# A two-stage convolution kernel put into one interleaved stage: a new sample order, two loads of every sample, band matrices on GpSimd, the output bias inside the expansion

## The chip, the cores and the metric

One core of a Trainium2 chip. The metric is the device time of one execution in microseconds; the kernel before took 1702.09 us, the median of three runs (1700.39 to 1702.37).

## What is computed

x has the shape (16, 64, 64, 768): 16 samples, 64 x 64 pixels, 768 channels, float32, 12.6 MB a sample. For each sample:

```
xn   = group_norm(x)                      # 32 groups of 24 channels, moments over all pixels of the sample
xc   = conv1x1(xn, conv1_w) + conv1_b      # 768 -> 16 channels
h    = mean(xc over pixels) @ H_w.T + H_b  # 4 logits a sample
g    = softmax over the top 2 of h         # (16, 4)
E_i  = downsample(conv3x3(upsample(xc, 2**i), convl_w) + convl_b),  i = 0..3
out  = x + conv1x1(sum_i gw[i, b] * E_i, conv2_w) + conv2_b
gw   = reshape(g, (4, 16))                 # a reshape, not a transpose
```

The reshape matters for the order of the work: the four gates of sample b come from row b // 4 of g's flat order, that is from the samples b//4, 4 + b//4, 8 + b//4 and 12 + b//4. Outputs of the samples 0 to 3 need the projections of 0, 4, 8 and 12, and no others.

## The kernel before

Everything runs on one core. A sample lies in SBUF as eight slots of 128 partitions x 3072 floats (1536 KB), each slot of four tiles of 128 pixels x 768 channels. There are twelve slots (x_low with 8, x_high with 4).

**First stage, all samples in order** (project_sample, copy_sample, take_stats, fold_norm). SyncE loads the slots; a load waits until the slot's last tenant is transposed. VectorE takes bn_stats of 30 of the 32 groups of a pair of slots (a chunk; four chunks a sample), ACT takes the other two groups by activations with accumulation. TensorE sums the moments over partitions with a matmul per chunk, and fold_norm turns them into scaled weights w1 by a dozen small VectorE instructions. For each of 24 steps (chunk c, block k of 128 channels) TensorE does eight transposes (L403) into one of three PSUM banks, ACT copies them to xT (L533), and TensorE projects them with four matmuls (L413) into img_ps. Transposes run LEAD = 6 steps ahead of projections, into the next sample too; statistics of the next sample run beside the projection of this one. ACT copies the 16-channel image with its bias to xc (L559), which keeps all 16 images. The loop turns over three samples at a time.

**Middle.** Logits, softmax and gates for all samples; the taps of the four experts; weights for the output.

**Second stage, samples 15, 0, 1, ..., 14** (expand_sample, add_sample, split_sample, store_and_reload). The last sample is still in SBUF, the other 15 are loaded again. Per sample VectorE weighs the taps (L820, L822) and makes seven band matrices (L828); TensorE convolves with 35 matmuls (70 records, L473), a quarter behind each of the slots 3 to 6 of the sample before. ACT and VectorE split the result into a high and a low float32r half (L599, L850), TensorE spreads them (L486, L487), ACT copies them to es4 (L603). For each of 32 tiles TensorE does four matmuls: two that write the output bias (L500, ones times b2) and two with the expansion (L501), 512 and 256 columns each. VectorE adds the tile to x in its slot (L867), and SyncE stores a slot when its four tiles are added, then reloads it (L321, L265). Eight slots are in use; the queue holds a wait for each.

SyncE issues all transfers, in program order, on one queue: a transfer whose wait is not met holds back those behind it. In the same way each engine works through its own order.

Of the kernel before, what the change touches and what calls it, by code (L numbers as in the profile page):

```python
# [12 lines left out]
P = 128  # L27
B, HH, WW, D = 16, 64, 64, 768
R, E = 16, 4
G = 32  # L30
# [6 lines left out]
TILES = HH * WW // P  # L37
SPS = TILES // QN
CHUNKS = SPS // 2
SLOTS = 12  # L40
LOW = 8
TURNS = 3
LOOPS = (B - 1) // TURNS
STEPS = CHUNKS * KB
XT_PS = 3
XT = 6
LEAD = KB
GV = G - 2
STATS_BUFS = 2
HALF = 2 * QN * CG // 2  # L50
SUMS_AT = [4, 9, 14, 19]

SCALAR_AT = [at + g for at in (1, 6, 11, 15) for g in range(G - GV)]
FOLD_OPS = 9
AHEAD_SUM = 4
AHEAD_DEVIATION = 3
AHEAD = AHEAD_SUM + AHEAD_DEVIATION + 8
GN_EPS = 1e-5
# [7 lines left out]
MAT_MASK = [SAME, SAME, SAME, ABOVE, BELOW, FIRST, LAST]  # L66

# [28 lines left out]
def slot_place(i):  # L96

    return (i // 2) % 2, 2 * (i // 4) + i % 2


# [15 lines left out]
MAT_ORDER = [HERE, UP, DOWN, FROM_ABOVE, FROM_BELOW, TOP, BOTTOM]  # L116

MATS_AT = 2
MATS_BEFORE = [MAT_ORDER[:1], MAT_ORDER[1:3], MAT_ORDER[3:5], MAT_ORDER[5:]]

CONV = [(m, a) for m in MAT_ORDER for a in (MID, LEFT, RIGHT, LEFT_EDGE, RIGHT_EDGE)]


def program(nc, x, conv1_w, conv1_b, convl_w, convl_b, conv2_w, conv2_b, H_w, H_b, out):
# [3 lines left out]
    coef = resize_taps()  # L128

    ctx = ExitStack()  # L130
    scratch = ExitStack()
    with ctx:
# [5 lines left out]


        x_low = sb("x_low", [P, LOW, QN, D])  # L140
        xc = sb("xc", [P, B, PIX])
        ident = sb("ident", [P, P])
        pooled = sb("pooled", [P, B])
        small = sb("small", [P, 3, G])


        x_high = sb("x_high", [P, SLOTS - LOW, QN, D], stack=scratch)
        xT = sb("xT", [P, XT, QN, 2 * P], stack=scratch)
        unread_copy = sb("unread_copy", [P, 2 * QN, CG], BF16, stack=scratch)
        w1T = sb("w1T", [P, KB, R], stack=scratch)  # L150
        w1_first = sb("w1_first", [P, KB, 2, 2 * R], stack=scratch)
        group_sum = sb("group_sum", [P, G], stack=scratch)
        group_of = sb("group_of", [P, 2, KB // 2, G // 2], stack=scratch)
        picked = sb("picked", [P, 2, KB // 2, G // 2], stack=scratch)


        stats = sb("stats", [P, STATS_BUFS, G, 6], stack=scratch)
# [50 lines left out]
        def slot(n):  # L208
            return x_low[:, n] if n < LOW else x_high[:, n - LOW]

# [51 lines left out]
        def _(sp):  # L262
# [3 lines left out]

            def load_sample(loop, turn, first):

                for i in range(SPS):
# [627 lines left out]
```

## Time and profile before

| | before |
|---|---|
| median of three runs | 1702.09 us |
| span of the profiled execution | 1703.1 us |
| its own time | none is listed beside the span |
| moved | 390.60 MB read, 201.33 MB written |
| mean | 348 GB/s |
| granted TensorE clock, mean | 0.909 |

The span goes from the first to the last instruction. "Busy" of TensorE is modelled from its pipelined instructions. The DMA share is the mean busy share of the core's 16 DMA engines; in saturated stretches it reads 1.02 to 1.03, since packets overlap a little. Times are in microseconds from the span's start.

### The profile page before, as it was taken

How to read it: one execution, taken by the hardware profiler on the slowest of the kernel's cores; microseconds unless marked ns; L12 is line 12 of the kernel's file. 1: busy time of each engine (PE TensorE's matmuls, PEld its weight loads, DVE VectorE, ACT ScalarE, POOL GpSimd, SP SyncE). 2: the span in 40 equal slices, each digit the busy share in tenths (PEclk: the TensorE clock that was granted, in tenths of full speed). 3: DMA queues.
4: the chain of work that ended last, by engine and by line, in shares of the span. 5: the costliest groups of instructions: out<-in, count | busy, mean ns of one | idle time of the engine just before them, and what ended most of it. 6: DMA issues, size and time to landing. Idle time of an engine off the chain costs nothing.

```text
span 1703.1 us, 28023 instructions
## 1 busy us (share of the span) xinstructions
PE 1399.3 (82%) x9584; PEld 991.1 (58%) x9584; DVE 1188.5 (70%) x3092; ACT 528.5 (31%) x1028; POOL 8.1 (0%) x28
## 2 busy tenths in 40 slices
PE   2799999999999999788897688778768767868862
PEld 2566666666666666466665466556556555656652
DVE  6988888788879887657666656655665664655642
ACT  3577777677777777300000000000000000000000
POOL 0000000000000001000000000000000000000000
PEclk7899999999999999889999898889799879879876
DMA  9888888788888882049999999999999999999999
GB/s 361 315 302 315 313 316 315 275 315 304 298 312 317 301 317 93 1 176 410 416 415 415 417 415 415 417 415 412 415 414 411 403 402 402 402 405 410 399 409 367
DMA packets 203029, 593.24 MB, mean 348 GB/s; under 512 B 10290, under 2 KB 10290, under 8 KB 202932
## 3 DMA queue, kind: packets, MB, share of 16 engines
q1 hardware_dynamic: 202932, 591.95, 89.3%
q8 instruction: 60, 0.98, 0.2%
q14 instruction: 37, 0.30, 0.1%
HBM read 390.60 MB, written 201.33 MB: 348 GB/s over the span
## 4 chain that ended last, share of the span: by engine, by line
PE 48%; DMA 28%; SPq 13%; DVE 6%; issue 3%; ACT 1%; DVEq 0%; ACTq 0%
PE xT_ps L403 22%; DMA out<-x_low 19%; PE img_ps L413 13%; DMA x_low<-in_x 9%; SPq L321 7%; SPq L265 6%; PE img_ps L473 5%; PE xT_ps L500 3%; DVE x_low L867 3%; PE xT_ps L501 2%; PE misc_ps L423 2%; DVE stats L678 2%; ACT xc L559 1%; ACT xT L533 0%; DVE taps L822 0%
## 5 line engine op out<-in xcount | busy, mean ns | idle before, releaser
L867 DVE TENSOR_TENSOR x_low<-x_low,xT_ps 128x768 f32<-128x768 f32 x512 | 470.2, 951 | 322.5 <-PE xT_ps L501 191.0
L500 PE MATMUL xT_ps<-b,all_one 128*128 128x512 f32 (+1 forms) x1024 | 430.5, 424 | 205.3 <-DVE x_low L867 204.6
L533 ACT COPY xT<-xT_ps 128x1024 f32<-128x1024 f32 x384 | 387.4, 1009 | 174.3 <-PE img_ps L413 172.2
L678 DVE BATCH_NORM_STATS2 stats<-x_low 128x6 f32<-128x192 f32 x1320 | 355.9, 344 | 68.6 <-DMA x_low<-in_x 51.4
L500 PEld LDWEIGHTS xT_ps<-b,all_one 128*128 128x128 f32 x1024 | 226.3, 221 | 281.0 <-DVE x_low L867 232.4
L501 PE MATMUL xT_ps<-w,es 128*128 128x512 f32 (+1 forms) x1024 | 376.6, 384 | 0.0
L403 PE MATMUL xT_ps<-ident,x_low 128*128 128x128 f32 x2112 | 291.9, 283 | 24.8 <-DMA x_low<-in_x 11.5
L403 PEld LDWEIGHTS xT_ps<-ident,x_low 128*128 128x128 f32 x2112 | 235.1, 143 | 117.2 <-ACT xT L533 60.4
L599 ACT ACTIVATE es_hi<-img_ps,bias_es 128x512 fp32r<-128x512 f32 x16 | 11.0, 688 | 799.1 <-PE img_ps L473 799.1
L501 PEld LDWEIGHTS xT_ps<-w,es 128*128 128x128 f32 x1024 | 231.5, 226 | 30.6
L473 PE MATMUL img_ps<-xc,band 128*128 (+6 forms) x1120 | 219.4, 343 | 4.2 <-DVE band L828 4.2
L473 PEld LDWEIGHTS img_ps<-xc,band 128*128 128x128 f32 x1120 | 157.4, 196 | 67.3 <-issue 62.9
L678 DVE BATCH_NORM_STATS2 stats<-x_high 128x6 f32<-128x192 f32 x600 | 162.0, 344 | 11.7 <-DMA x_high<-in_x 11.5
L413 PE MATMUL img_ps<-xT,xc 128*32 128x256 f32 x1920 | 153.4, 391 | 8.4 <-ACT xc L559 8.4
L403 PE MATMUL xT_ps<-ident,x_high 128*128 128x128 f32 x960 | 130.0, 278 | 0.0
L403 PEld LDWEIGHTS xT_ps<-ident,x_high 128*128 128x128 f32 x960 | 104.4, 141 | 41.6 <-ACT xT L533 28.0
L413 PE MATMUL img_ps<-xT,w_first 128*32 128x256 f32 x1152 | 92.3, 396 | 2.1 <-ACT xc L559 2.1
L828 DVE TENSOR_TENSOR band<-taps,masks 128x640 f32<-128x640 f32 x112 | 87.6, 820 | 0.6
L413 PEld LDWEIGHTS img_ps<-xT,xc 128*32 128x32 f32 x1920 | 37.8, 108 | 49.3 <-issue 32.5
L603 ACT CAST es<-xT_ps 128x512 fp32r<-128x512 f32 x64 | 34.6, 589 | 70.1 <-PE xT_ps L487 70.1
L423 PE MATMUL misc_ps<-stats,ones 128*128 128x192 f32 x128 | 39.2, 391 | 20.6 <-ACT xc L551 7.7
L423 PEld LDWEIGHTS misc_ps<-stats,ones 128*128 128x128 f32 x128 | 20.0, 196 | 46.5 <-issue 24.7
(105 smaller groups left out, 432.5 us busy)
## 6 DMA issues: line engine op xcount, KB each, us to landing
x_low<-in_x SPq DMA_DIRECT2D x208, 1536.0 KB, 11.8
out<-x_low SPq DMA_DIRECT2D x128, 1536.0 KB, 18.0
x_high<-in_x SPq DMA_DIRECT2D x40, 1536.0 KB, 9.9
x_high<-in_L_conv_conv_w SPq DMA_DIRECT2D x8, 48.0 KB, 10.2
bias<-in_L_conv_conv_b SPq DMA_DIRECT2D x8, 0.1 KB, 9.9
wl_raw<-in_L_conv_convl_w SPq DMA_DIRECT2D x8, 9.0 KB, 1.9
bias_l<-in_L_conv_convl_b SPq DMA_DIRECT2D x8, 0.1 KB
gate_w<-in_L_conv_H_w SPq DMA_DIRECT2D x8, 0.2 KB
```

The lines of the kernel that those rows point to most:

```text
L265: sp.dma_start(slot(n), x_v[sample, p, j]).then_inc(loaded[n], 16)
L321: sp.dma_start(out_v[sample, p, j], slot(i)).then_inc(stored[i], 16)
L403: last = nc.tensor.transpose(xT_ps[:, buf, q, half * P:(half + 1) * P], slot((SPS * turn + 2 * c + half) % SLOTS)[:, q, k * P:(k + 1) * P] ...
L413: last = nc.tensor.matmul(img_ps[32 * q:32 * q + 32, 2 * P * (c // 2):2 * P * (c // 2 + 1)], w1[turn][:, k, c % 2, :], xT[:, n % XT, q, :] ...
L423: nc.tensor.matmul(misc_ps[:, 0:6 * G], ones[:, :], stats[:, c % STATS_BUFS].rearrange("p g t -> p (g t)"), start=(c == 0), stop=(c == CHU ...
L473: last = nc.tensor.matmul(img_v[:, blk_out, col_out], band[:, m, ax].rearrange("p h r -> p (h r)"), xc_v[:, order, blk_in, col_in], start= ...
L500: nc.tensor.matmul(add_ps[:, n % 2, part], all_one[:, :], b2[:, part], start=True, stop=False)
L501: last = nc.tensor.matmul(add_ps[:, n % 2, part], es4[:, q, j * P:(j + 1) * P], w2[:, p, part], start=False, stop=True)
L533: nc.scalar.copy(xT[:, n % XT], xT_ps[:, n % XT_PS]).then_inc(xT_copied, 1)
L678: ins = nc.vector.bn_stats(stats[:, c % STATS_BUFS, g, :], tiles[:, :, g * CG:(g + 1) * CG])
L828: nc.vector.tensor_tensor(band[:, m], taps[:, MAT_ROW_TAP[m]].unsqueeze(2).broadcast_to(full), masks[:, MAT_MASK[m]].unsqueeze(1).broadcas ...
L867: nc.vector.tensor_tensor(slot(i)[:, q, :], slot(i)[:, q, :], add_ps[:, n % 2, :], ALU.add).then_inc(added, 1)
```

## The change

The two stages become one list of 22 units, and all loops are written out. A unit (a, b) projects sample a and makes the output of sample b side by side; either can be None. One function, orders(), writes the order of TensorE, ACT and VectorE; the order of the transfers is written out by hand. L is the first load of a slot, R its second, S its store; "L4.0:0" loads slot 0 of sample 4 into place 0 of 12.

```diff
+UNITS = [(4, None), (8, None), (12, None), (0, None), (1, 0), (2, 1), (3, 2), (9, 3), (13, None), (5, None),
+         (6, 5), (7, 6), (14, 7), (10, 4), (11, 10), (15, 11), (None, 15), (None, 8), (None, 9), (None, 12),
+         (None, 13), (None, 14)]
+KEPT = {}
+TRANSFERS = """
+L4.0:0 L4.1:1 L4.2:2 W1 L4.3:3 L4.4:4 L4.5:5 L4.6:6 L4.7:7 L8.0:8 L8.1:9 L8.2:10 L8.3:11 L8.4:6
...
+L6.7:8 R5.1:10 R5.2:3 R5.3:4 L7.0:6 R5.4:8 S5.0 S5.1 L7.1:5 R5.5:11 S5.2 L7.2:9 L7.3:10 S5.3
+R5.6:3 L7.4:0 R5.7:1 S5.4 L7.5:4 S5.5 L7.6:2 R6.0:7 L7.7:8 S5.6 R6.1:11 S5.7 R6.2:3 R6.3:1
+L14.0:2 R6.4:8 S6.0 S6.1 L14.1:0 R6.5:4 S6.2 L14.2:7 L14.3:11 S6.3 R6.6:3 L14.4:9 R6.7:10 S6.4
+L14.5:1 S6.5 L14.6:5 R7.0:6 L14.7:8 S6.6 R7.1:4 S6.7 R7.2:3 R7.3:10 L10.0:5 R7.4:8 S7.0 S7.1
...
+S15.7 R8.3:6 R8.4:7 R8.5:11 S8.0 S8.1 S8.2 S8.3 S8.4 S8.5 R8.6:5 R8.7:10 R9.0:3 R9.1:9
+R9.2:1 S8.6 S8.7 R9.3:4 R9.4:0 R9.5:8 R9.6:2 S9.0 S9.1 S9.2 S9.3 S9.4 S9.5 S9.6
```

The sizes, and the order of the steps (chunk 3, the slots 6 and 7, is transposed first):

```diff
-XT = 6
-LEAD = KB
-GV = G - 2
-STATS_BUFS = 2
+XT = 4
+LEAD = 2
+XC = 6
+BANDS = 4
+GV = G - 4
+TILE_PAIRS, TILE_PAIRS_LOADED = 10, 12
+GROUPS_FROM, GROUPS_FROM_LOADED = 6, 4
+LATE_SUM_PART = 4
+def step_chunk(n):
+    return CHUNKS - 1 - n // KB, n % KB
```

The body of orders(), for one unit. "late" holds where this unit and the sample are both in play: then the last chunk's statistics, the fold and the first two transposes of a stand at the start of its own unit.

```diff
+    def tile(b, t):
+        pe.append(("tile", b, t))
+        dve.append(("add", b, t))
+        if t == 13:
+            spread(b, 2)
+        if t == 15:
+            spread(b, 3)
...
+        if due is not None:
+            pe.append(("logits", due))
+            act.append(("exponent", due))
+            dve.append(("softmax", due))
+            dve.append(("gates", due))
+        if is_late:
+            for c in range(CHUNKS - 1):
+                pe.append(("sum", a, c))
+            statistics(a, CHUNKS - 1, range(GV))
+            fold(a)
+        if due is not None:
+            pe.append(("gates", due))
+        if b is not None:
+            for part in range(NM):
+                pe.append(("conv", b, part))
+                if is_late and part == LATE_SUM_PART:
+                    pe.append(("sum", a, CHUNKS - 1))
+            act.append(("high", b))
+            dve.append(("low", b))
+            for part in range(2):
+                spread(b, part)
+        if is_late:
+            for n in range(LEAD):
+                transpose(a, n)
+        if a is None:
+            for t in range(TILES):
+                tile(b, t)
+            continue
+        per_pair, groups, done, summed = tiles_by_pair(u), groups_by_pair(u), 0, 0
+        for m in range(STEPS // 2):
+            tiles = list(range(done, done + per_pair[m]))
+            done += per_pair[m]
+            for place, n in enumerate((2 * m + LEAD, 2 * m + LEAD + 1, 2 * m, 2 * m + 1)):
+                if place >= 2:
+                    pe.append(("project", a, n))
+                elif n < STEPS:
+                    transpose(a, n)
+                elif following is not None and not late(u + 1):
+                    transpose(following, n - STEPS)
+                for t in tiles[place * len(tiles) // 4:(place + 1) * len(tiles) // 4]:
+                    tile(b, t)
...
+            for c in range(CHUNKS):
+                part = [g for of, g in groups[m] if of == c]
+                if part:
+                    statistics(following, c, part)
```

So a unit's 32 tiles are spread over its 12 pairs of steps, 84 groups of the next sample's first three chunks over pairs 4 to 11. Transposes, tiles and spreads share three PSUM banks in turn (ring_ps, three of 1024 columns). The loads and stores, TensorE's tile and GpSimd's bands:

```diff
+            def load(kind, s, i):
+                n, _, before = loads[kind, s, i]
+                if before is not None:
+                    was, s0, i0 = before
+                    if was == "L" and i0 >= KEPT.get(s0, 0):
+                        sp.wait_ge(transposed, AI[s0] * STEPS + (CHUNKS - i0 // 2) * KB)
+                    else:
+                        sp.wait_ge(stored[n], 16 * stores[n])
+                sp.dma_start(x_sb[:, n], x_v[s, i // 4, i % 4]).then_inc(loaded[n], 16)
...
-                    for part in (slice(0, 512), slice(512, D)):
-                        nc.tensor.matmul(add_ps[:, n % 2, part], all_one[:, :], b2[:, part], start=True, stop=False)
-                        last = nc.tensor.matmul(add_ps[:, n % 2, part], es4[:, q, j * P:(j + 1) * P], w2[:, p, part],
-                                                start=False, stop=True)
+                for part in (slice(0, 512), slice(512, D)):
+                    last = nc.tensor.matmul(flat_ps[:, buf, part], es4[:, q, (i % 4) * P:(i % 4 + 1) * P], w2[:, part],
+                                            start=True, stop=True)
...
+            def weigh_taps(b, bi):
...
+                for e in range(E):
+                    g, of_e = gates[:, b, e:e + 1], experts[:, e].rearrange(flat)
+                    if e == 0:
+                        link(nc.gpsimd.tensor_scalar(all_e, of_e, g, None, ALU.mult))
+                    else:
+                        part = band[:, NM * bi % BANDS].rearrange("p a h r -> p (a h r)")[:, 0:NT * NT * R]
+                        link(nc.gpsimd.tensor_scalar(part, of_e, g, None, ALU.mult))
+                        link(nc.gpsimd.tensor_tensor(all_e, all_e, part, ALU.add))
...
+                    nc.gpsimd.tensor_tensor(band[:, n % BANDS], taps[:, MAT_ROW_TAP[m]].unsqueeze(2).broadcast_to(full),
+                                            masks[:, MAT_MASK[m]].unsqueeze(1).broadcast_to(full),
+                                            ALU.mult).then_inc(band_ready, 1)
```

The output bias sits in rows 64 to 127 of w2, against rows of es4 that are kept at one. es4 has the spread values in its first 64 partitions only, and is copied in four parts of 64 x 1024. The expert taps are computed on GpSimd too. xc keeps six images. ACT takes four groups of a chunk, VectorE 28. Gates are computed in four rounds, when a = 0, 5, 10 and 15 is projected.

## Rows read from the trace of the kernel before

**Rows 1.** The page: busy time of each engine over the span.

```profile
PE 1399.3 (82%) x9584; PEld 991.1 (58%) x9584; DVE 1188.5 (70%) x3092; ACT 528.5 (31%) x1028; POOL 8.1 (0%) x28
```

**Rows 2.** Projections of line 413: durations, first and last start.

```profile
L413 PE MATMUL img_ps<-xT,w_first x1152: 379/379/637, 55.0 to 703.6; 128*32 128x256 f32 x192
```

**Rows 3.** Stretches: length, busy PE, PEld, DVE, ACT, POOL, then clock, DMA share, GB/s.

```profile
20.00:45.00 25.00, 4.34 (x20) 2.86 (x18) 23.73 (x94) 7.00 (x26) 0.00 (x0) 0.58 1.03 387
...
58.00:700.00 642.00, 624.37 (x6130) 403.07 (x6128) 535.38 (x2180) 462.75 (x901) 5.28 (x14) 0.99 0.76 283
708.00:733.00 25.00, 17.48 (x74) 11.93 (x75) 15.40 (x30) 0.69 (x1) 0.00 (x0) 0.70 0.00 1
...
800.00:1340.00 540.00, 422.20 (x1874) 320.84 (x1875) 343.30 (x404) 25.54 (x45) 0.00 (x0) 0.89 1.03 415
1340.00:1690.00 350.00, 256.35 (x1100) 196.43 (x1099) 199.86 (x231) 14.19 (x25) 0.00 (x0) 0.84 1.02 404
```

**Rows 4.** Waits in total: us, times, longest; the last row the DMA queue's.

```profile
PE xT_ps L500 <- DVE x_low L867: 204.6, 141, 6.2
DVE x_low L867 <- DMA x_low<-in_x: 131.2, 43, 8.0
...
SPq L265 <- DMA out<-x_low: 340.4, 58, 8.2
```

**Rows 5.** Timeline of the first stage: start, length, engine, line; a step and a fold.

```profile
643.55 1.09 PE L403 MATMUL xT_ps<-ident,x_high 128*128 128x128 f32 x8
...
644.57 0.64 PE L413 MATMUL img_ps<-xT,xc 128*32 128x256 f32 x8
...
645.14 1.09 PE L403 MATMUL xT_ps<-ident,x_high 128*128 128x128 f32 x8
...
648.33 0.59 PE L423 MATMUL misc_ps<-stats,ones 128*128 128x192 f32 x2
...
652.45 7.89 DVE L678 BATCH_NORM_STATS2 stats<-x_low 128x6 f32<-128x192 f32 x30 [1.28 <-DMA x_low<-in_x]
...
665.63 0.36 DVE L711 TENSOR_REDUCE small<-misc_ps 128x96 f32<-128x192 f32 x1 [5.00 <-PE misc_ps L423]
...
668.99 0.42 DVE L737 TENSOR_TENSOR w_first<-w1T,of_channel 128x96 f32<-128x96 f32 x2
```

**Rows 6.** Timeline at a turn of the first stage's loop.

```profile
550.77 1.09 PE L403 MATMUL xT_ps<-ident,x_low 128*128 128x128 f32 x8 [2.28 <-issue]
```

**Rows 7.** Timeline of the second stage, at full clock: one tile, and a quarter convolution.

```profile
795.15 0.50 PE L500 MATMUL xT_ps<-b,all_one 128*128 128x512 f32 x1 [0.16 <-DVE x_low L867]
...
796.03 0.51 PE L500 MATMUL xT_ps<-b,all_one 128*128 128x512 f32 x1
...
808.42 5.51 PE L473 MATMUL img_ps<-xc,band 128*128 x18
```

**Rows 8.** Groups by line: count, then busy us and mean ns, then idle before.

```profile
L867 DVE TENSOR_TENSOR x_low<-x_low,xT_ps 128x768 f32<-128x768 f32 x512 | 470.2, 951 | 322.5 <-PE xT_ps L501 191.0 <-DMA x_low<-in_x 131.2
...
L828 DVE TENSOR_TENSOR band<-taps,masks 128x640 f32<-128x640 f32 x112 | 87.6, 820 | 0.6
...
L355 POOL TENSOR_SCALAR_AFFINE_SELECT masks<-masks 128x128 f32<-128x128 f32 x10 | 3.6, 358 | 0.7
...
L375 POOL MEMSET masks<- 128x640 f32 x1 | 0.6, 632 | 0.0
```

**Rows 9.** Timeline of the middle: first tap, first convolution, low half.

```profile
711.10 0.42 DVE L820 TENSOR_SCALAR taps<-experts,gates 128x400 f32<-128x400 f32 x1
...
714.45 15.93 PE L473 MATMUL img_ps<-xc,band 128*128 128x512 f32 x70 [4.24 <-DVE band L828]
...
731.24 0.75 DVE L850 SCALAR_TENSOR_TENSOR es_lo<-img_ps,bias_es,es_hi 128x512 fp32r<-128x512 f32 x1 [7.15 <-ACT es_hi L599]
```

**Rows 10.** Timeline of the start: first loads issued, first statistics.

```profile
0.81 3.40 SPq L265 DMA_DIRECT2D x_low<-in_x  x4
...
11.48 7.89 DVE L678 BATCH_NORM_STATS2 stats<-x_low 128x6 f32<-128x192 f32 x30 [11.48 <-DMA x_low<-in_x]
```

More of the change, by code:

```diff
@@ L113, in blk_ranges, with row_due, late @@
             BOTTOM: (slice(NB - 1, NB), slice(NB - 1, NB))}[m]
[L116 to L121, printed above, removed]
+def step_chunk(n):
+    return CHUNKS - 1 - n // KB, n % KB
+def row_due(u):
+    a = UNITS[u - 1][0] if u else None
+    return a // 5 if a is not None and a % 5 == 0 else None
+def late(u):
+    return u < len(UNITS) and None not in UNITS[u]
@@ new lines, in tiles_by_pair, with groups_by_pair @@
+def tiles_by_pair(u):
+    b = UNITS[u][1]
+    if b is None:
+        return [0] * (STEPS // 2)
+    last = TILE_PAIRS if KEPT.get(b, 0) else TILE_PAIRS_LOADED
+    ends = [min(TILES, -(-TILES * (m + 1) // last)) for m in range(STEPS // 2)]
+    return [end - start for start, end in zip([0] + ends, ends)]
+def groups_by_pair(u):
+    a, following = UNITS[u][0], (UNITS[u + 1][0] if u + 1 < len(UNITS) else None)
+    out = [[] for _ in range(STEPS // 2)]
+    if following is None or a is None:
+        return out
+    chunks = 3 if late(u + 1) else 4
+    b = UNITS[u][1]
+    first = 0 if b is None else GROUPS_FROM if KEPT.get(b, 0) else GROUPS_FROM_LOADED
+    last = 12 if late(u + 1) else 11
+    every = [(c, g) for c in range(chunks) for g in range(GV)]
+    for n, item in enumerate(every):
+        out[first + n * (last - first) // len(every)].append(item)
+    return out
@@ new lines, with psum_turns, image_places @@
+PE_ORDER, ACT_ORDER, DVE_ORDER = orders()
+def psum_turns():
+    turn = {}
+    for work in PE_ORDER:
+        if work[0] in ("transpose", "tile", "spread", "weights_2", "logits"):
+            turn[work] = len(turn)
+    return turn
+TURN = psum_turns()
+TURNS = list(TURN)
+def image_places():
+    place, before, free, held = {}, {}, [(n, None) for n in range(XC)], {}
+    for a, b in UNITS:
+        if b is not None:
+            free.append((held.pop(b), b))
+        if a is not None:
+            place[a], before[a] = free.pop(0)
+            held[a] = place[a]
+    return place, before
@@ L630, in expert_taps @@
+            for part in range(2):
+                ins = nc.gpsimd.tensor_tensor(row_kind[:, part:part + 1], masks[:, SAME, part, 0:1],
+                                              masks[:, SAME, 2 + part, 0:1], ALU.add)
+            ins.then_inc(masks_ready, 1)
             def expert_taps():
@@ new lines, in _ @@
+            for work in DVE_ORDER:
+                if work[0] == "groups":
+                    groups(*work[1:])
+                elif work[0] == "add":
+                    add(*work[1:])
+                elif work[0] == "fold":
+                    fold(*work[1:])
+                elif work[0] == "low":
+                    low_half(*work[1:])
+                elif work[0] == "softmax":
+                    softmax(*work[1:])
+                elif work[0] == "gates":
+                    take_gates(*work[1:])
+                elif work[0] == "weights_1":
+                    weights_1()
+                else:
+                    weights_2()
```

1055 lines of the change are left out of this document (539 added, 516 removed).

## The prediction

> **What bounds the kernel now.** I read, in this order, busy time by engine, the stretches of the span, the waits of the engines and of the DMA queue, then single operations in the timeline. The whole-span shares say little, since the kernel has two stages with different limits [rows 1]. In the first, from the first projection at 55.0 us to the last at 703.6 us [rows 2], TensorE is busy 624 of 642 us at a granted clock of 0.99, while the DMA engines stand at 0.76 [rows 3]: 648.6 / 16 = 40.5 us a sample, TensorE's own work. In the middle nothing moves for some 30 us: DMA share 0.00 [rows 3]. In the second stage the DMA share is 1.03 at 415 GB/s, later 1.02 at 404 [rows 3]; TensorE waits 205 us for additions, VectorE 131 us for loads, and the queue itself waits 340 us for stores to free slots [rows 4]. That stage is bound by transfers: 16 of 1.573 MB (1536 KB) a sample, 3.79 us each at 415 GB/s, 60.6 us. So one stage is TensorE's and one is the DMA's, and the change lays the first over the second.
>
> **Prices of a transfer.** Reads alone, with DMA share 1.03, ran at 387 GB/s [rows 3]: 4.06 us each. Alternating reads and stores cost 3.79, so a store is worth 2 x 3.79 - 4.06 = 3.52. A unit that loads a sample, reloads another and stores it has two reads per store: (2 x 4.06 + 3.52) / 3 = 3.88 us, bounded by 3.79 and 4.06. The changed kernel moves 256 loads and 128 stores (8 loads more than before). If the DMA never idled that would be 256 x 4.06 + 128 x 3.52 = 1490 us; all depends on how long it idles.
>
> **Units.** UNITS has 22: six with a projection only (4, 8, 12, 0, 13, 5), ten with both, six with an output only.
>
> *Projection only.* A step is 8 transposes and 4 projections, 1.59 us from one to the next, 24 of them 38.2 us; four moment sums at about 0.52 make 40.3 [rows 5]. The fold, statistics to weights, is 665.63 to 669.41, 3.8 us [rows 5]. Before, six transpose steps ran ahead of it; now the last sum stands behind the last projection and only two steps are ahead, two more transposes cover 2.0 us, and some 2.2 us of TensorE idle remain: 42.5 us a unit. VectorE needs only 4 x 7.4 + 4.8 = 34 us (30 groups take 7.89 us [rows 5], 28 take 7.4). The DMA would need 8 x 4.06 = 32.5, so it idles 10 us in each. The deleted loops save a little: at a turn of the loop TensorE stood 2.28 us [rows 6]; there are three such places, so at most 7 us. I count nothing. The Trainium skill (Runtime: NRT & Kernel Launch, Instruction fetch mechanics) says why: code is fetched strictly ahead in blocks and a taken branch can fall outside them, while straight code hides its fetches. The trace agrees so far that the loop's bodies show no such stall.
>
> *Both.* TensorE: 40.3 for the projection; convolution 9.6 (18 of 70 matmuls, 2873 of 4992 columns, in 5.51 us [rows 7]); tiles: four matmuls with 1536 columns take 796.03 - 795.15 = 0.88 us [rows 7], so two with 768 about 0.44, 32 of them 14; spreads 16 x 0.29 = 4.6: together 68.5. Removing the bias matmuls halves the tile, 14 us a sample of TensorE time, but TensorE was not the limit where they stood. VectorE: 4 x 7.4 for groups, 32 x 0.92 = 29.4 for additions (470.2 / 512 [rows 8]), 5 for fold and low half: 64. The ACT engine (copies, twice the groups, es4) stays near 45. Transfers: 24 x 3.88 = 93. On busy times alone the DMA bounds this unit at 93 us.
>
> But a serial stretch is added, and here I choose. Twelve slots hold the eight of sample a and four of b. In the hand-written order every unit ends: load a'.7, store, load, store, two loads; then the next transfer is load a''.0, which needs the slot of a'.6, free only after six transpose steps of the next unit. Those can't begin before all of a' is loaded and its last two slots are through statistics, fold and, by program order on VectorE and TensorE, the low half and two spreads. From the landing of a'.7: groups 7.4; scaling, semaphores and the moment matmul (0.59 [rows 5]) 1.3; fold 3.8; low half 0.75 [rows 9] and hand-overs 1.1; two spreads 2.0: 15.6 us. Then six transpose steps with two projections and three tiles: 6 x 1.02 + 2 x 0.57 + 3 x 0.44 = 8.6, and 0.9 for the three shared PSUM banks: 9.5. From issue to data the idle queue costs 2.4 (two slots, the first issued at 0.81, are there at 11.48 [rows 10]: 10.7 - 8.1). From a''.0 to a''.7 lie 19 transfers in the table, 73.7 us. Cycle: 15.6 + 9.5 + 2.4 + 73.7 = 101.2 us. After a'.7 five transfers are left, 19.4 us, against 27.5 of the stretch: DMA idle 8 us a unit. Inside the 19 I find no stall: store b.6 and the transposes of chunk 0 are each ready some 10 us before their place.
>
> The granted clock adds to it. After 10 us of idle TensorE the convolution at 714.45 took 15.93 us [rows 9], against 9.6 at full clock: 6.3 more. TensorE idles before the spreads and waits for tiles at a unit's end, so the stretch costs 0 to 7 us more; in the second stage the mean clock was 0.84 to 0.89 [rows 3], nearer to the good end. I take 3: T = 104.
>
> *A gate row is due* ahead of units with b = 0, 5, 10 and 15. From the last projection (703.6) to VectorE's first tap (711.10) are 7.5 us [rows 2, 9]. Then GpSimd weighs taps in seven linked operations of 400 elements and makes five bands before the last moment sum. The trace has no tensor_tensor on GpSimd. From below, a memset of 640 elements takes 0.63 us; from above, affine_select of 128 takes 0.358, 1.79 for 640 in proportion [rows 8]; VectorE's own was 0.82 per band. I take 1.3 per band and 0.85 per weighing, between them (5.95 + 6.5 = 12.5, bounds 6 and 17). With part four 2.3, sum 1.0, fold 3.8, low 1.1, spreads 1.8: 30 us from last projection to first transpose. At b = 10 it replaces 21, so 9 more; at b = 15 the DMA has a backlog. In the other units the first bands are made during the unit before, and the last three lie beside 5.7 us of convolution: nothing. The Trainium skill (GPSIMD Engine Reference, 3.1 Elementwise — side-by-side cycle accounting) has 4497 ns for 2048 elements, two inputs, by which I estimate 1.4 us a band; no run here shows it yet.
>
> *Output only.* 16 x 3.79 = 60.6 us of transfers against 14 of convolution, halves and copy and 29.4 of additions. The slots let loads run during the first part. It stays transfer-bound as before.
>
> **The sum, against the profiled execution** (span 1703.1 us; no other time is listed for it, and it stands 1 us above the median of the runs, 1702.09). First projection at 52 (55.0, less four chunks with two fewer groups and the groups that stood inside the first fold). Four units of 42.5, and 2 for the second weights: 224. Gate row 30: 254. Three cycles of 104: 566. Unit (9, 3) ends by the landing of its 18th transfer, 12 + 70, then groups and fold, 92: 658. Two units of 42.5: 743. Gate row 30: 773. Three cycles: 1085. One with 9 more: 1198. One more: 1302. Then 108 transfers are left (R11.4 on): 10 + 108 x 3.79 + 8 for the last addition and its store = 427: 1729. Less 1: 1728 us.
>
> So the merged stages gain the middle gap and nearly all of the first stage's DMA idling by share, but lose it again: six units at 10, eight boundaries at 11, start and gates.
>
> **Rivals.**
> 1. *The queue stays fed* (not slower). In-flight loads cover the boundary and T is the bare 93. For it: in the second stage a DMA share of 1.02 to 1.03 was held with eight slots only [rows 3]. Against it: slot a'.6 is needed first and comes last. 1729 - 8 x 11 - 9 = 1632. It decides from a stretch under 19 us.
> 2. *TensorE at the lower clock* through each stretch and the transposes that free slots: T = 111, 8 x 7 = 56 more: 1785. For it 15.93 against 9.6 us [rows 9, 7]; against it the mean clock of 0.84 to 0.89 [rows 3].
> 3. *GpSimd is much slower* than its rows (5 us a band): then convolution waits everywhere, about 10 us a unit over 13 more units with outputs: 1859.
> 4. *Code fetch*. By the skill's rule above loops cost and straight code doesn't: 1721 by the three stalls of 2.28 us.
>
> **Chances.** Forecast, with rival 4, 0.53 (own range 1690 to 1770: rate of a transfer 3.79 to 4.06 is -14 to +27, clock -24 to +32, GpSimd +-15); rival 1 0.29; rival 2 0.12; rival 3 0.06. Range: 1632 to 1790. 0.2% (3.4 us) is about what can be told from no change. Faster: rival 1, and 0.06 of the forecast's low end, 0.35. Same 0.05. Slower 0.60.
>
> **What would show it.** The DMA share in mixed units 0.90 to 0.93 with a hole of 8 to 11 us at each boundary; about 104 us from unit to unit; TensorE's spreads waiting for the low half behind the fold; units without output 42.5 us; the last 400 us at 415 GB/s. I am wrong if the share stays at 1.0 across boundaries (rival 1), if slots of b rather than a.6 are awaited, or if band operations take over 2 us.

## The result and the profile after

The changed kernel takes 1813.2 us (median of four runs, 1809.4 to 1815.9) against 1702.2 (1700.4 to 1703.1): ratio 1.0663, 95% interval 1.0638 to 1.0688. It is slower, as forecast, but by 111 us where 26 were forecast, and 23 us above the upper end of the range. The profiled execution has a span of 1809.0 us and a granted clock of 0.839.

The page of the changed kernel, to be laid beside [rows 1] and [rows 3]; in the strips each character is 45.2 us:

```profile
PE 1264.0 (70%) x8700; PEld 856.3 (47%) x8700; DVE 1072.3 (59%) x2763; ACT 668.1 (37%) x1549; POOL 351.8 (19%) x359
...
PEclk9999888888887878978798787977888899768876
DMA  9698719979698888928959789795796999999998
GB/s 364 233 359 313 279 65 409 362 278 410 233 411 343 346 320 314 341 75 321 411 225 411 305 339 411 276 410 237 274 409 267 413 408 414 406 413 412 412 411 358
```

TensorE is busy 135 us less than in [rows 1], with half of each tile's matmuls gone, and the kernel is no faster for it. The DMA strip shows why: full slices alternate with gaps, twice down to 65 and 75 GB/s (the gate rows), and only from 1402 us on does it stay near 411, up to the last slice. Laid over the transfers one by one, the queue moves nothing for 12 to 18 us at each boundary of two units, for 43 us at each of the two full gate rows and for 31 us at the third. One unit with both, cut into its stretches (columns as in [rows 3]):

```profile
899.00:926.00 27.00, 19.88 (x82) 13.10 (x83) 16.58 (x48) 5.01 (x19) 18.58 (x14) 0.76 0.65 259
926.00:934.00 8.00, 8.00 (x72) 6.62 (x71) 2.86 (x3) 5.49 (x6) 0.22 (x1) 1.00 0.00 0
934.00:990.00 56.00, 42.62 (x329) 29.12 (x327) 34.41 (x76) 24.90 (x52) 0.00 (x0) 0.85 1.01 393
990.00:1010.00 20.00, 9.00 (x63) 5.36 (x62) 13.67 (x35) 5.79 (x20) 0.00 (x0) 0.83 1.03 412
1010.00:1037.00 27.00, 18.48 (x83) 12.62 (x84) 17.88 (x54) 5.02 (x19) 18.77 (x14) 0.77 0.71 282
```

The last load of the coming sample (its slot 7) lands at 898.9 and again, one unit on, at 1011.3. From 934 to 1010 the DMA is full (1.01 and 1.03), as forecast; in the 27 us behind a landing it runs out (0.65), and it stands at 0.00 while six transpose steps empty slots. Now those 27 us in the timeline (start, length, engine, line, idle before):

```profile
899.02 0.24 DVE L929 SCALAR_TENSOR_TENSOR stats<-stats 128x56 f32<-128x56 f32 x1
899.17 7.36 DVE L925 BATCH_NORM_STATS2 stats<-x_sb 128x6 f32<-128x192 f32 x28
...
899.31 1.00 PE L696 MATMUL misc_ps<-stats,ones 128*128 128x192 f32 x2 [5.54 <-DVE stats L929]
...
900.11 13.25 PE L734 MATMUL img_ps<-xc,band 128*128 128x512 f32 x50
...
913.21 0.57 PE L696 MATMUL misc_ps<-stats,ones 128*128 128x192 f32 x2
...
913.82 0.36 DVE L935 TENSOR_REDUCE small<-misc_ps 128x96 f32<-128x192 f32 x1 [6.35 <-PE misc_ps L696]
914.07 1.03 POOL L626 TENSOR_TENSOR taps<-taps,band 128x400 f32<-128x400 f32 x1
914.22 0.93 DVE L937 TENSOR_TENSOR norm<-small 128x32 f32<-128x32 f32 x1
915.07 0.18 DVE L938 TENSOR_TENSOR norm<-small 128x32 f32<-128x32 f32 x1
...
920.06 1.77 DVE L956 TENSOR_TENSOR w<-w1T,of_channel 128x96 f32<-128x96 f32 x2
920.20 6.03 POOL L639 TENSOR_TENSOR band<-taps,masks 128x640 f32<-128x640 f32 x4
921.87 0.75 DVE L995 SCALAR_TENSOR_TENSOR es_lo<-img_ps,bias_es,es_hi 128x512 fp32r<-128x512 f32 x1
...
922.72 0.66 PE L751 MATMUL ring_ps<-es_hi,pick 128*64 128x512 f32 x1 [6.81 <-issue]
...
926.02 3.66 PE L673 MATMUL ring_ps<-ident,x_sb 128*128 128x128 f32 x32
```

To be read upward from 926.02. The first transposes stand behind eight spreads (3.3 us), these behind the low half, this behind a fold of 8.0 us (913.82 to 921.87; 3.8 in [rows 5]), this behind the last moment sum at 913.21. That sum is queued on TensorE behind 50 convolution matmuls of 13.25 us, and they are queued behind the third moment sum at 899.31, which waited 5.54 us for the statistics of the third chunk. VectorE was through with the last chunk at 907.5 and then waited 6.35 us for a sum that TensorE could not reach.

Four things therefore lie in the stretch: the hold in front of the convolution, the convolution, the fold and the low clock. The experiments take the fold, the hold, the loads and the clock one by one; the convolution itself was not shortened in any run.

### The profile page after: what moved, and what is told of

Its sections match the earlier page's. It is cut to its first block, busy times and chain, and to the rows that moved or that the text cites. A ratio compares the mean times of both kernels' runs of the same rounds, so it can differ in the third digit from the quotient of the medians.

```text
span 1809.0 us, 23732 instructions
## 1 busy us (share of the span) xinstructions
PE 1264.0 (70%) x8700; PEld 856.3 (47%) x8700; DVE 1072.3 (59%) x2763; ACT 668.1 (37%) x1549; POOL 351.8 (19%) x359
## 4 chain that ended last, share of the span: by engine, by line
PE 44%; DMA 22%; DVE 17%; ACT 6%; issue 5%; SPq 3%; POOL 2%; ACTq 0%; DVEq 0%; POOLq 0%
DMA x_sb<-in_x 22%; PE ring_ps L673 13%; PE img_ps L734 11%; DVE x_sb L1005 8%; PE img_ps L686 7%; PE ring_ps L763 7%; DVE stats L925 6%; PE ring_ps L751 2%; ACT unread_squares L820 2%; PE ring_ps L752 2%; ACT unread_copy L822 2%; SPq L489 2%; ACT xT L803 1%; PE misc_ps L696 1%; SPq L498 1%
## 5 line engine op out<-in xcount | busy, mean ns | idle before, releaser
L1005 DVE TENSOR_TENSOR x_sb<-x_sb,ring_ps 128x768 f32<-128x768 f32 x512 | 470.1, 950 | 353.4 <-PE ring_ps L763 274.4
L925 DVE BATCH_NORM_STATS2 stats<-x_sb 128x6 f32<-128x192 f32 x1792 | 477.1, 344 | 135.3 <-DMA x_sb<-in_x 134.9
L763 PE MATMUL ring_ps<-w,es 128*128 128x512 f32 (+1 forms) x1024 | 339.2, 426 | 291.8 <-ACT xT L803 190.8
L803 ACT COPY xT<-ring_ps 128x1024 f32<-128x1024 f32 x384 | 367.9, 1013 | 189.8 <-PE ring_ps L673 189.4
L673 PE MATMUL ring_ps<-ident,x_sb 128*128 128x128 f32 x3072 | 409.0, 291 | 32.3 <-DMA x_sb<-in_x 18.1
L673 PEld LDWEIGHTS ring_ps<-ident,x_sb 128*128 128x128 f32 x3072 | 378.3, 151 | 73.5 <-issue 44.9
L763 PEld LDWEIGHTS ring_ps<-w,es 128*128 128x128 f32 x1024 | 177.3, 216 | 442.2 <-ACT xT L803 208.6
L639 POOL TENSOR_TENSOR band<-taps,masks 128x640 f32<-128x640 f32 x112 | 168.9, 1533 | 847.1 <-PE img_ps L734 845.8
L734 PE MATMUL img_ps<-xc,band 128*128 128x1 f32 (+8 forms) x1120 | 236.4, 365 | 45.2 <-POOL band L639 45.2
L686 PE MATMUL img_ps<-xT,w 128*32 128x256 f32 x3072 | 235.2, 407 | 11.0 <-DVE w L956 10.6
L686 PEld LDWEIGHTS img_ps<-xT,w 128*32 128x32 f32 x3072 | 73.8, 112 | 100.4 <-ACT xT L803 39.0
L935 DVE TENSOR_REDUCE small<-misc_ps 128x96 f32<-128x192 f32 x16 | 5.7, 358 | 106.8 <-PE misc_ps L696 106.8
## 6 DMA issues: line engine op xcount, KB each, us to landing
x_sb<-in_x SPq DMA_DIRECT2D x256, 1536.0 KB, 14.6
```

Source lines behind the costliest of these rows:

```text
L639: nc.gpsimd.tensor_tensor(band[:, n % BANDS], taps[:, MAT_ROW_TAP[m]].unsqueeze(2).broadcast_to(full), masks[:, MAT_MASK[m]].unsqueeze(1). ...
L673: last = nc.tensor.transpose(ring_ps[:, buf, q, half * P:(half + 1) * P], slot("L", a, 2 * c + half)[:, q, k * P:(k + 1) * P], ident[:, :])
L686: last = nc.tensor.matmul(img_ps[32 * q:32 * q + 32, 2 * P * (c % 2):2 * P * (c % 2 + 1)], w1[:, AI[a] % 2, k, c // 2, :], xT[:, at % XT, ...
L734: last = nc.tensor.matmul(img_v[:, blk_out, col_out], band[:, n % BANDS, ax].rearrange("p h r -> p (h r)"), xc_v[:, XC_PLACE[b], blk_in, c ...
L763: last = nc.tensor.matmul(flat_ps[:, buf, part], es4[:, q, (i % 4) * P:(i % 4 + 1) * P], w2[:, part], start=True, stop=True)
L803: nc.scalar.copy(xT[:, at % XT], ring_ps[:, TURN["transpose", a, n] % RING]).then_inc(xT_copied, 1)
```

## The experiments

Each is compared with the kernel before on the same chip; "cycle" is the time between the high halves (es_hi) of two neighbouring units with both, without the one that holds a gate row. There are seven. In the changed kernel they are 110.8 to 112.4, 111.7 on the mean. "The stretch" goes from the landing of slot 7 to the first transposes: 27.1 us at 899.

**GpSimd's work moved off the fold.**

```
     pool.wait_ge(band_used, NM * bi - BANDS + 1)
+    pool.wait_ge(lo_ready, bi)
     weigh_taps(b, bi)
```

> GpSimd starts to weigh the taps of the next output only when VectorE has taken the low half of the present one, so that no GpSimd work lies beside the fold. Theory (the changed kernel's cycle is the landing of L a.7, then a serial stretch of 25 us up to the next transposes, six transposes, 19 transfers; the fold in it takes 8.0 us instead of 3.8 because GpSimd and VectorE hold each other up): fold back to 3.8 to 4.5 us, its ten occurrences shorter by 4 us each beside an output, of which 8 or 9 count: 1775 to 1785 us. Rival (the order of the transfers or ACT's waits set the time, the fold is off the path): within 5 us of 1813.

1786.7 us, ratio 1.0504 (1.0486 to 1.0522), 26 us less than the changed kernel, just above what I expected; cycle 107.0 to 108.7, 108.0 on the mean. The timeline has the same instructions with nothing beside them:

```profile
899.33 0.36 DVE L936 TENSOR_REDUCE small<-misc_ps 128x96 f32<-128x192 f32 x1 [4.86 <-PE misc_ps L697]
899.72 0.19 DVE L938 TENSOR_TENSOR norm<-small 128x32 f32<-128x32 f32 x1
...
902.61 0.16 DVE L955 TENSOR_TENSOR bias<-bias,sums 128x1 f32<-128x1 f32 x1
902.68 0.42 DVE L957 TENSOR_TENSOR w<-w1T,of_channel 128x96 f32<-128x96 f32 x2
903.14 0.75 DVE L996 SCALAR_TENSOR_TENSOR es_lo<-img_ps,bias_es,es_hi 128x512 fp32r<-128x512 f32 x1
```

The fold is 3.8 us again, from 899.33 to 903.14. So GpSimd beside VectorE cost 4.2 us a fold. In the changed kernel seven of the ten folds beside an output are that long; the three ahead of a gate row have no weighing beside them and take 3.8. The cycle is 3.7 us shorter on the mean.

**The first three moment sums behind part 4 of the convolution.**

```
-        for c in range(CHUNKS - 1):
-            pe.append(("sum", a, c))
...
     if is_late and part == LATE_SUM_PART:
-        pe.append(("sum", a, CHUNKS - 1))
+        for c in range(CHUNKS):
+            pe.append(("sum", a, c))
```

> In the units with both, the moment sums of the first three chunks stand with the fourth behind part 4 of the convolution, so that the convolution starts with the image and not with the third chunk's statistics. Theory: convolution starts about 6 us earlier, the last moment sum comes some 4 us earlier in the seven or so units where no gate row is due: 1780 to 1790 us. Rival (the convolution isn't on the path, the stretch is VectorE's): no change.

1790.1 us, ratio 1.0521 (1.0499 to 1.0542), 23 us less; cycle 106.8 to 109.7, 108.7 on the mean. The hold in front of the convolution is real, and this run understates it. The fold now starts 9.8 us behind the landing of slot 7 (893.3), where it was 14.9 in the changed kernel. But it lies beside more of GpSimd's bands and takes 9.7 us (903.14 to 912.83) instead of 8.0:

```profile
903.14 0.36 DVE L934 TENSOR_REDUCE small<-misc_ps 128x96 f32<-128x192 f32 x1 [0.69 <-PE misc_ps L695]
...
906.17 6.04 POOL L638 TENSOR_TENSOR band<-taps,masks 128x640 f32<-128x640 f32 x4
...
907.84 1.44 DVE L945 TENSOR_TENSOR norm<-norm,small 128x32 f32<-128x32 f32 x1
909.20 1.62 DVE L947 TENSOR_TENSOR picked<-norm,group_of 128x96 f32<-128x96 f32 x1
...
912.83 0.75 DVE L994 SCALAR_TENSOR_TENSOR es_lo<-img_ps,bias_es,es_hi 128x512 fp32r<-128x512 f32 x1
```

So 5 us are won ahead of the fold and 1.6 lost in it.

**The last load of a sample one place earlier, and one place later.** In the eight units with the pattern below; the first line is the changed kernel, then the two edits.

```
 L.6 R.0 L.7 S.6
 L.6 L.7 R.0 S.6     earlier
 L.6 R.0 S.6 L.7     later
```

> In the table of transfers, L a.7 changes places with the load of the other sample directly before it, in eight units; the transfers are the same. Theory: one transfer fewer between the first transposes and the landing of L a.7, 3.9 us in each of eight cycles: 1780 to 1785 us. Rival (what bounds is the rate of the DMA, or the waits for additions and stores): no change, since the same bytes move in the same time.

> The changed kernel, with slot 7's load one place later in eight units (behind the store of slot 6 instead of ahead of it): the opposite of the run in which it stood one place earlier and nothing came of it. Theory (the landing of slot 7 and the end of VectorE's groups of chunk 2 stood at the same moment, so earlier gains nothing, but later costs): 4 to 5 us in each of eight cycles, 1843 to 1855 us. Rival (the places of these transfers don't matter): within 5 us of 1813.

Earlier: 1818.5 us, ratio 1.0686 (1.0663 to 1.0710). Later: 1817.7 us, 1.0683 (1.0668 to 1.0699). Both are some 5 us above the changed kernel, with intervals that overlap its own. An earlier load gained nothing and a later one cost hardly anything: my theory of a critical slot 7 falls. Of the second kernel, around the last chunk:

```profile
1017.10 0.24 DVE L926 SCALAR_TENSOR_TENSOR stats<-stats 128x56 f32<-128x56 f32 x1
1020.75 7.36 DVE L922 BATCH_NORM_STATS2 stats<-x_sb 128x6 f32<-128x192 f32 x28 [3.42 <-DMA x_sb<-in_x]
1028.14 1.22 DVE L926 SCALAR_TENSOR_TENSOR stats<-stats 128x56 f32<-128x56 f32 x1
...
1031.31 0.57 PE L693 MATMUL misc_ps<-stats,ones 128*128 128x192 f32 x2
...
1031.92 0.36 DVE L932 TENSOR_REDUCE small<-misc_ps 128x96 f32<-128x192 f32 x1 [2.56 <-PE misc_ps L693]
```

VectorE now waits 3.42 us for the load, but only 2.56 us for the sum, where it waited 6.35 at 913.82: the wait has moved, the sum has not. The sum comes about 14 us behind the third chunk's statistics in each kernel (899.26 to 913.21 in the changed one; 1017.34 to 1031.31 here), with the convolution between. So slot 7 had 5.7 us of room (907.5 to 913.2). With slot 7 earlier VectorE began its groups 4.1 us behind the landing instead of 0.3, since the third chunk's came first. That leaves the third chunk, which slot 5 completes, as what holds the sum; VectorE did wait 2.87 us for slot 5 at 883.61, but also 3.5 us for tiles behind it, and no run moved slot 5 alone.

**ACT's groups behind VectorE's in every unit.**

```
-        if groups[0] == 0:
+        if groups[-1] + 1 == GV:
             for g in range(GV, G):
                 act.append(("scalar_group", a, c, g))
```

> ACT's four groups of a chunk are put behind VectorE's last piece of that chunk and not ahead of its first, so that ACT no longer stands waiting for the two loads with copies behind it. Theory: TensorE's waits for ACT's copies (191 us in total) go, but they lie in the part of the cycle that the transfers set: within 10 us of 1813. Rival (ACT's head-of-line wait holds up transposes, additions and stores, and by that the queue): 5 us or more in each of ten units, 1750 to 1770 us.

1849.1 us, ratio 1.0870 (1.0842 to 1.0898): slower, against both expectations. The cycle fell to 106.9 to 109.6, but the first high half came at 293.5 instead of 244.1: the four units without an output ahead of it grew by some 12 us each. That ACT's copies are needed at once there is my reading of the order; no run takes it apart. From here on the edit is kept to samples whose own unit has both.

**Taps weighed on VectorE.** Four instructions behind the low half (or behind the gates) in place of GpSimd's seven; GpSimd keeps the bands.

```
+                    if e == 0:
+                        link(nc.vector.tensor_scalar(all_e, of_e, g, None, ALU.mult))
+                    elif e < E - 1:
+                        link(nc.vector.scalar_tensor_tensor(all_e, of_e, g, all_e, ALU.mult, ALU.add))
...
```

> One part undone: the taps of the experts are weighed on VectorE again (four instructions, behind the low half of the output before, or behind the gates where a row is due); GpSimd keeps the bands. Theory: no GpSimd work beside the fold, as in the run where GpSimd waits (-26 us), and four gate rows get their taps in 2.5 instead of 8.9 us, three of them on the path: 1765 to 1775 us. Rival (the wait alone had done all): about 1787.

1767.6 us, ratio 1.0398 (1.0374 to 1.0422), 46 us less, the largest of the single edits; first high half at 238.0 instead of 244.1. The weighing by GpSimd in the changed kernel, and by VectorE here:

```profile
217.73 1.28 POOL L622 TENSOR_SCALAR taps<-experts,gates 128x400 f32<-128x400 f32 x1 [79.69 <-DVE bias_es L990]
...
225.46 1.02 POOL L626 TENSOR_TENSOR taps<-taps,band 128x400 f32<-128x400 f32 x1
226.56 5.96 POOL L639 TENSOR_TENSOR band<-taps,masks 128x640 f32<-128x640 f32 x4
...
228.23 4.56 PE L734 MATMUL img_ps<-xc,band 128*128 128x512 f32 x5 [11.36 <-POOL band L639]
```

```profile
217.87 0.43 DVE L1014 TENSOR_SCALAR taps<-experts,gates 128x400 f32<-128x400 f32 x1
218.34 1.31 DVE L1016 SCALAR_TENSOR_TENSOR taps<-experts,gates,taps 128x400 f32<-128x400 f32 x2
219.68 0.64 DVE L1018 SCALAR_TENSOR_TENSOR taps<-experts,gates,taps 128x400 f32<-128x400 f32 x1
...
222.16 10.10 PE L739 MATMUL img_ps<-xc,band 128*128 128x512 f32 x35 [5.07 <-POOL band L644]
```

8.8 us against 2.5 ahead of the convolution of every gate row. This run also takes the weighing off the fold, so its 46 us hold the 26 of the run in which GpSimd waits; the other 19 lie mostly at three gate rows, each 6 us shorter than in that run.

**Three edits together** (GpSimd behind the low half, sums behind part 4, ACT's groups late in mixed units).

> GpSimd's wait for the low half, the moment sums behind part 4 of the convolution, and ACT's groups behind VectorE's last piece of a chunk, this last only where the following unit has both. Theory (fold, convolution and moment sum stand in one stretch, so that shortening both counts more than either): cycle 101 instead of 111.5 us, 1725 to 1740 us. Rival (the stretch's parts hide each other, gains of 26 and 23 don't add): 1775 or more.

1761.5 us, ratio 1.0367 (1.0342 to 1.0391): 52 us less, where the first two alone sum to 50. It lies between my two expectations. Either ACT's order adds little here or the gains overlap; this run can't tell. The stretch is down to 18.0 us and the cycle to 103.4 to 105.4, 104.3 on the mean: the forecast's 18.6 and 104. And now the landing of slot 7 binds, VectorE waiting 2.4 to 3.2 us for it at seven of the eight boundaries:

```profile
981.74 7.37 DVE L925 BATCH_NORM_STATS2 stats<-x_sb 128x6 f32<-128x192 f32 x28 [3.12 <-DMA x_sb<-in_x]
```

**The same, with slot 5 loaded ahead of R.7 and S.4, and slot 7 ahead of R.0.**

> The same, and in eight units the load of slot 5 of the sample coming up stands ahead of a load and a store that were in front of it, and slot 7's ahead of the load in front of it. Theory (VectorE's groups of chunk 2 begin with slot 5, and those of chunk 3 come only behind them, which is why slot 7 alone brought nothing): 3 to 4 us a cycle under the run with the three together, 1695 to 1715 us. Rival (with the stretch shortened the DMA's own rate binds, 93 us a cycle, or the loads displaced are missed as much): within 5 us of that run.

1725.8 us, ratio 1.0146 (1.0120 to 1.0172), 36 us less; cycle 99.2 to 101.2, 100.0 on the mean, so 4.2 us less. It is above the range that I expected, since the run with the three stood above its own. The stretch stays at 18.0; slot 7 lands one transfer earlier in the cycle. It fits the reading above, but does not prove it: slot 7 alone was not moved in this state. There VectorE had waited 2.4 to 3.2 us for it, so by itself it could have given that much of the 4.2, and only the rest needs slot 5.

**The kernel before, without its bias matmuls** (line 500; the bias is left out of the result), to price this part of the change alone.

> The kernel before without its two bias matmuls a tile (the output bias is left out of the result). Theory: its second stage is bound by transfers, so half of the tile's TensorE time is worth nothing there: within 5 us of before. Rival (TensorE's tiles hold up additions and so stores): 10 to 40 us faster.

1693.8 us, ratio 0.9962 (0.9946 to 0.9977). Half of each tile's matmuls are worth 6 us where they stood, just over the 5 that I allowed (the mean granted clock is 0.803 without them, 0.909 with them).

**Building it up.** First the four edits together (weighing on VectorE, sums late, ACT late in mixed units, slots 5 and 7 earlier); then loads 6 and 7 also ahead of S.5; then the sums behind the whole convolution (LATE_SUM_PART = 6).

> The taps weighed on VectorE, the moment sums behind part 4 of the convolution, ACT's groups behind VectorE's last piece, and the loads of slots 5 and 7 earlier: all that shortened the cycle, together. Theory (what was gained at gate rows, 20 us by weighing on VectorE instead of only waiting, adds to the run with earlier loads, 1726): 1700 to 1710 us, the kernel before's time. Rival (VectorE's 2.5 us more a unit lie on the path): 1720 or more.

> As the one before, and in eight units the loads of slots 6 and 7 stand ahead of the store of slot 5. Theory (the landing of slot 7 gates again, since chunk 3's groups waited 4.8 us for it while chunk 2's were done): one transfer fewer in front of it, up to 3.9 us a cycle, 1675 to 1690 us. Rival (the queue stands longer waiting for slot 4's store, or the DMA's own rate of 93 us binds): within 8 us of the run before.

> As that, and all four moment sums stand behind the whole convolution (part 6). Theory: the convolution is done before chunk 3's statistics, so the high half is ready and only fold, low half and spreads follow the sum: 1 us a cycle less, 5 to 10 us. Rival (TensorE then idles about 10 us ahead of the spreads and runs them and the first transposes at 1.2 GHz): 10 to 25 us slower than the run before.

1708.9 us, ratio 1.0055 (1.0040 to 1.0071); 1695.1 us, 0.9966 (0.9955 to 0.9978); 1692.3 us, 0.9951 (0.9933 to 0.9969). The last beats both kernels, by 0.5% and by 6.7%; its 3 us against the second can't be told from nothing by the intervals. The cycle is 99.9 to 101.4, 96.9 to 99.7, then 96.0 to 98.3; on the mean 100.4, 98.5 and 96.7. The second run gave 2.0 us a cycle of the 3.9 expected and missed its range. The stretch 850 to 1250 of the changed kernel and of the last one:

```profile
850.00:1250.00 400.00, 273.68 (x1854) 185.86 (x1855) 248.90 (x639) 147.44 (x352) 56.31 (x42) 0.82 0.89 352
```

```profile
850.00:1250.00 400.00, 303.98 (x2172) 205.63 (x2172) 268.02 (x695) 167.69 (x387) 42.33 (x28) 0.86 0.97 378
```

**TensorE kept busy in the stretch.** The last kernel with 16 and 24 unread matmuls of 128x128 around the sums of every mixed unit.

```
+    pe.append(("warm", b, 16))
     for c in range(CHUNKS):
         pe.append(("sum", a, c))
+    pe.append(("warm", b, 24))
```

> The fastest version so far (1692 us), with 16 matmuls of 128 columns ahead of the moment sums and 24 behind them in each unit with both; nothing reads their results. They fill TensorE's wait for statistics, fold and low half. Theory (the serial stretch costs more than its instructions since TensorE comes out of its idle at 1.2 GHz: convolution 14.3 instead of 9.6 us, spreads and first transposes about half slower): spreads and first transposes at 2.4 GHz, 2 to 4 us a cycle, 1660 to 1680 us. Rival (the DMA is busy 98% in the cycles, so that nothing is left to win; or the fillers don't raise the clock and only delay): 1690 or more.

1693.3 us, ratio 0.9961 (0.9949 to 0.9973), outside the 1660 to 1680 that I expected. First the spreads without the fillers, then with them:

```profile
955.46 0.63 PE L752 MATMUL ring_ps<-es_hi,pick 128*64 128x512 f32 x1
```

```profile
950.22 5.52 PE L783 MATMUL ring_ps<-ident 128*128 128x128 f32 x48
955.49 0.47 PE L754 MATMUL ring_ps<-es_hi,pick 128*64 128x512 f32 x1
955.80 0.40 PE L755 MATMUL ring_ps<-es_lo,pick 128*64 128x512 f32 x1
...
850.00:1250.00 400.00, 330.30 (x2516) 241.41 (x2515) 270.47 (x706) 166.59 (x387) 42.37 (x28) 0.92 0.98 380
```

The fillers did what they were to do to the clock: 0.92 instead of 0.86, the eight matmuls of two spreads in 1.9 us instead of 3.2, and stretches of 15.4 to 16.2 us instead of 16.6 to 16.9. But the DMA share goes from 0.97 to 0.98 only. The cycle is 94.2 to 96.8, 95.4 on the mean, 1.3 us less where 2 to 4 were expected; one of the seven is 0.8 longer. At 24 transfers of 3.88 us, my estimate, a cycle would be 93, and these are within 1 to 4 of that. What the seven cycles gain, 9 us, is mostly lost at the two later gate rows (109.1 to 113.4 for the cycle that holds one, and 226.8 to 230.0 for the span with the other), where the fillers stand too. So in this state the clock is worth little. Fillers away from the gate rows were not tried.

## Why the prediction was right in sign and short in size

**Right, the frame.** The steps outside the boundary came out nearly to the microsecond. From the first transposes at 926.02 to the landing of slot 7 at 1011.3 are 85.3 us; the terms 9.5 + 2.4 + 73.7 give 85.6. Its parts are each some 1.5 off and cancel: 8.0 us to the next issue at 934.03, and 77.3 from there. The last unit with both begins its transposes at 1378.8, and the rest takes 430 us for 427. The six projection-only units cost less than forecast at the start (last projection at 211.8, not 224) and what was forecast behind unit (9, 3) (686.0 to 771.5, 85.5 for 85). The first transposes at 253.8 meet the forecast 254, but by two errors of 12 us that cancel. The DMA holes lie at the boundaries, as stated, but are 12 to 18 us long and not 8 to 11. The three loop turns of 2.28 us are too small to be told apart in these sums.

**Failed: the serial stretch, "15.6 us", with 3 for the clock.** It measured 27.0 us from 899.0, and 25.7 from 1011.3 (next first transposes at 1036.99). First an error of my own sum: its terms, 7.4, 1.3, 3.8, 0.75, 1.1 and 2.0, make 16.35. The rest, term by term against the first of the two:
- groups to the start of the fold: 14.8 against 8.7. I saw the last sum wait for the last statistics and took TensorE as free by then. It was not: the convolution stands ahead of it, itself held by the third sum. With the sums moved it is 9.2 to 9.8 us; the slot-7 runs show that it, not the landing, binds.
- fold: 8.05 against 3.8. I took the duration from [rows 5], where GpSimd was idle, and priced GpSimd's new work only by how long it takes, not by what it does to VectorE. This is the term that a trace of before could not show; the run with GpSimd moved shows it at 4.2 us.
- low half and hand-overs: 0.85 against 1.85.
- spreads: 3.3 against 2.0, the low clock, inside the 3 us allowed.

Together 10.7 us over the terms as they stand. With the first two undone, in the run with three edits, the stretch is 18.0 us and the cycle 104.3: the forecast's T.

**Failed: the gate row, "30 us".** It took 42 (211.8 to 253.8). GpSimd's weighing was 8.8 us for 5.95 expected, a band 1.53 for 1.3 (inside the bounds). But the main part is again the convolution. From the end of the weighing (226.6) to the last sum (241.1) are 14.6 us, of which 13.05 are its first 50 matmuls; I had counted 6.5 for five bands and "part four 2.3", 8.8, as if the parts before it hid behind GpSimd. The low clock explains only a little of this: it was granted up to 232.9 and costs some 2.3 us there.

```profile
228.30:232.80 4.50, 4.50 (x6) 1.94 (x7) 0.00 (x0) 0.00 (x0) 4.22 (x3) 0.50 0.01 4
233.00:241.00 8.00, 8.00 (x44) 5.64 (x43) 0.00 (x0) 0.00 (x0) 6.19 (x5) 1.00 0.00 0
```

Then the fold, doubled as above.

**Mis-sized: the convolution, "9.6".** I scaled one quarter, 5.51 us, by columns. At a granted clock of 1.00 all of it takes 12.9 us, and the four quarters of one sample before, each at 1.00 too, take 5.51 + 3.68 + 2.12 + 1.84 = 13.1 (from 756.97 on): the later quarters hold many short matmuls.

```profile
1492.91 12.87 PE L734 MATMUL img_ps<-xc,band 128*128 128x512 f32 x70
```

So of the 15.93 us in [rows 9] only some 3 are the clock's, and not the 6.3 of the prediction, and the unit's TensorE sum of 68.5 is 3 short. This changed no term of the serial stretch, but it made the convolution look shorter than it is and the low clock dearer.

**Where the 80 us of the profile went** (1809 against a sum of 1729), by the first transposes of the units. At 253.8 for 254: 0. Three cycles on, 584.9 for 566: 19; the last of these boundaries has no weighing beside its fold, since a gate row is due. From there to the last projection (771.5) 186.6 for 177: 10, nearly all in unit (9, 3), 101 for 92. Gate row 42 for 30: 12. Three cycles, 813.5 to 1144.6, 331 for 312: 19. The cycle with the gate row, to 1271.0, 126.3 for 113: 13. The last, to 1378.8, 107.9 for 104: 4. The rest 3. The boundaries of the cycles carry most of it. The two later gate rows carry 25, with the boundary that one of them holds; what the first cost is hidden by the start.

**The rivals.** The fed queue (1632) needed a stretch under 19 us; here it had 27. In the best version the queue is fed across the boundaries, and is at rest at the gate rows:

```profile
221.00:259.00 38.00, 29.62 (x166) 20.75 (x166) 18.53 (x58) 8.43 (x11) 16.58 (x11) 0.79 0.00 1
737.00:774.00 37.00, 28.78 (x162) 20.35 (x166) 18.15 (x57) 7.79 (x11) 16.58 (x11) 0.84 0.00 1
```

The low-clock rival had 111 us a cycle, the measured length, and for the wrong reason: the clock accounts for about 1.3 us of the spreads and, granted at 0.50 from 898.5 to 905.3, for some 2.6 of the 13.25 of convolution (each an estimate, from the length of that stretch and the durations at either level); undoing two other causes, one at a time, gave 3.7 and 3.1 us a cycle, and the loads another 4.2. How much of the clock's part would come back in the changed kernel was not tried. GpSimd at 5 us a band: no; TensorE waited for bands only 45 us in total, at the four gate rows.

The range ended at 1790 because no case in it had two things late at one boundary. They add there, being links of one chain: undone singly, the work beside the fold gave 26 us and the hold 23, and together, with ACT's order, 52.

**Why the fold doubled.** The trace shows `norm<-small` of line 937 at 0.93 us beside GpSimd's tensor_tensor and 0.19 with GpSimd quiet, and at the end of GpSimd's instruction it ends too (915.10 and 915.15). The statistics (one input in SBUF, 7.36 us for 28 at 217.46, beside GpSimd, and at 899.17, without it) and the additions (one input in PSUM; the 31 that lie beside a GpSimd tensor_tensor took 0.95 us as the others did) kept their price. The Trainium skill (SBUF — State Buffer, "Who interferes with whom") states this: a VectorE instruction with two SBUF inputs contends with a GpSimd one that reads SBUF, and one with at most one does not. The trace agrees for GpSimd's tensor_tensor. Beside its tensor_scalar, which reads SBUF too, lines 939 and 945 grew (0.55 and 0.47 us for 0.19), while lines 944, 946 and 948 with two inputs kept 0.19, 0.19 and 0.25. The prediction did not weigh this rule against the fold; it speaks directly against moving work to GpSimd here.

**What beat the kernel before, and by how little.** The version at 1692.3 has the merged stages at a DMA share of 0.97 and is 8 us under the kernel before, in which leaving out the bias matmuls alone gave 6. It moves more bytes by eight loads, still fills the pipeline for 250 us before the first output, and pays two full gate rows with the queue at rest for 38 us each.

## What to carry to other kernels

When two stages are merged, write down what stands ahead of each instruction of the boundary on its own engine, not only what it waits for: here one matmul was queued behind a convolution that was itself queued behind a wait. Take no duration from a trace in which a newly used engine was idle; small two-input VectorE operations beside GpSimd's tensor_tensor took four to eight times as long. Price a convolution of many sizes from all of its records, not from the share of columns of its first part. And before a transfer is moved, ask which wait ends last: a load that is awaited in the profile can still have microseconds of room behind another link.

## What the runs showed of the hardware

- VectorE beside GpSimd's tensor_tensor: a 128x32 tensor_tensor 0.93 us for 0.19, a 128x1 one 0.95 for 0.16, two 128x96 1.77 for 0.42; with the sums moved, 1.44 for 0.19 and 1.62 for 0.25. Beside GpSimd's tensor_scalar it is less or nothing: 0.55 for 0.19 (line 939, 915.28), 0.19 for 0.19 (line 946, 918.40).
- On GpSimd a tensor_scalar of 128x400 took 1.28 us and a tensor_tensor of the same size, with one input more, 1.02 to 1.03. VectorE did the tensor_scalar in 0.43.
- 24 filler matmuls of 128x128 (48 records, 5.52 us) ahead of the spreads let these run at 0.40 us instead of 0.63: the granted clock is 1.00 from 950.2 to 957.4, and 0.50 from 952.0 to 955.4 without them, the 2.4 GHz level for the 1.2 GHz one. The kernel's time did not move.
- The convolution of 70 records takes 12.9 us at a granted clock of 1.00 and 15.6 to 15.8, with a moment sum of some 0.4 between its records, where the first 4.7 to 5.2 us are at 0.50.
